# A linear-attention and soft-MoE layer on one core: head pairs projected two at a time on the row halves of TensorE, one rms-normalised form transposed

## The chip, the cores and the metric
One core of a Trainium2 chip. The metric is the device time in microseconds of one execution; lower is better. The kernel has 16 batches of 256 tokens by 128 channels, all in float32 at its borders.

## The reference, cut to what matters
```python
xn = layernorm(x)                                   # (16, 256, 128)
# attention branch
q, k, v = split(xn @ Wqkv + bqkv)                   # 16 heads of 8
feat(t) = exp(clip(t/|t| @ omega * sqrt(2s) - s, -20, 20)) / sqrt(32) * sqrt(w)   # 64 features per head
ctx = causal_sum(qf . kf^T) v;  den = causal_sum(qf . kf^T);  a = ctx / max(den, 1e-6)
# expert branch
xr = rms_norm(xn, gamma_x);  se = rms_norm(slot_embeds, gamma_slot)               # 512 slots
logits = xr @ se^T;  dispatch = softmax over tokens-to-slots;  combine = softmax over slots
slots = dispatch^T @ xr;  h = gelu(slots @ w1);  out = combine @ (h @ w2)
return x + a @ Wout + bout + out
```

## The kernel before, in words
The batches run one after another in `run_rows`, a loop over pairs of batches with the first two and the last two written out. Each engine has its own `row(b, first, nxt, nxt2)`, an order written out by hand over 8 steps `s`. Step s belongs to head pair s of batch b, and beside it the pieces of the previous batch (bp) and the next one (b1) are placed. There is no planner: each engine takes its instructions in program order, and semaphores (`ft_ok`, `cl_ok`, `fe_ok`, ...) join the engines. `after` waits before an instruction; `hold` waits and puts a no-operation behind the wait.

The way of one head pair p: `project` (TensorE, L898) multiplies the stacked, normalised q and k (`stack_t`, 96 rows: high part, low part, high part) by the features' weights (`omega_st[:, p]`) in two matmuls of 256 columns into the one bank `p_feat`. `clip` (VectorE, L681) reads it into `arg`, `feature_exp` (ScalarE, L486) makes `feat`. `scores` (TensorE, L909) multiplies features of keys and queries, head by head on the two row halves, into `p_sa` and `p_sb`. `evac_a` (VectorE, L687) and `evac_b` (ScalarE, L491, then `mask_b` on GpSimd, L428) mask and store them. `context` (TensorE, L926) takes two pairs at a time (a = 0 to 3) into the bank `p_ctx`, where a = 0, 1, 2 add up in one half and a = 3 takes the other; `ctx_copy` (ScalarE, L496) copies each half once.

Because `p_feat` is one bank, each `project(b, p)` waits for the clip of pair p - 1. The projections are spread over the steps: pair 2 in step 0, 3 in step 1, 4 in step 2, 5 in step 3, 6 in step 4, 7 in step 5, and pairs 0 and 1 of the next batch in steps 6 and 7.

Around it in TensorE's order: step 0 `processed(bp)` (h @ w2, L1022), scores 0, `context(bp, 3)`, `transposes(b1)` (L878, L880: the layernormed `xn` and the rms-normalised `xg`, two tiles each), `ctx_transposed(bp)` (L939). Step 1 scores 1, `qkv_product(b1)` (L869), `combine(bp)` (L1032), `attn_back(bp)` (L945, waits for VectorE's `ctx_norm`, L694 to L707). Step 2 scores 2, `attention_out(bp)` (L951), `logits(b)` (L869, 6 matmuls of 512 columns for the tokens' form, 12 of 256 for the slots' form). Step 3 scores 3, `context(b, 0)`, `shift(b)` (L978, L986; needs the maxima of L714 and L720). Step 4 scores 4, `context(b, 1)`, `slot_sums` (L994). Step 5 scores 5, `slots_transposed` (L1002). Step 6 scores 6, `context(b, 2)`, `hidden` half 0 (L869). Step 7 scores 7, `hidden` half 1.

VectorE's order: step 1 `xt_low` (L653), clip 2, evac_a 1, `ctx_norm(bp)`. Step 2 `qkv_bias(b1)` (L661), clip 3, `add_experts(bp)`, evac_a 2, `add_attention(bp)`, `qk_norms(b1)`. Step 3 `token_maxima`, `slot_maxima`, clip 4, evac_a 3, `qk_newton`. Step 4 clip 5, evac_a 4, `ln_stats`. Step 5 clip 6, `slots_norm`, evac_a 5. Step 6 `slots_low` (L735), clip 7, evac_a 6, `ln_apply` of the batch after the next (L636 xn, L640, L647 xg). Step 7 clip 0 of the next batch, evac_a 7.

ScalarE's order in the steps that matter: step 4 `dispatch_exp`, evac_b 4, exp 5, `stack_high` (L479); step 5 `combine_exp`, evac_b 5, exp 6, `ln_root`; step 6 `slots_high` (L513), evac_b 6, exp 7; step 7 two gelus with a table load before and after, `ctx_copy(b, 0)`, exp 0 of the next batch, evac_b 7. SyncE issues the loads of x, the stores and `turn_stack`, a transposing DMA from `stack` to `stack_t`.

Of the kernel before, what the change touches and what calls it, by code (L numbers as in the profile page):

```python
# [16 lines left out]
PAIRS = HEADS // 2  # L17
# [67 lines left out]
def build(nc, x, Wqkv, bqkv, Wout, bout, omega, nodes, weights, gamma_x, gamma_slot, slot_embeds,  # L85
          w1, w2, out):
    with ExitStack() as ctx:
# [23 lines left out]
        gx_bc = sb("gx_bc", [128, 128])  # L111
        gs_bc = sb("gs_bc", [128, 128])
# [8 lines left out]
        node_b = sb("node_b", [32, R])  # L121
        node_b2 = sb("node_b2", [32, R])
        om_scale = sb("om_scale", [32, R])
# [6 lines left out]
        omega_f = sb("omega_f", [32, PAIRS, 128])  # L130
        omega_st = sb("omega_st", [96, PAIRS, 128], F16)

# [6 lines left out]
        xn = sb("xn", [128, TILES, C])  # L139
        junk = sb("junk", [128, NCH, C])  # L140
        xg = sb("xg", [128, 2, TILES, C + 1])
        xt_hi = sb("xt_hi", [128, 2, 512], F32R)
        xt_lo = sb("xt_lo", [128, 2, 512], F32R)
# [3 lines left out]
        stack = sb("stack", [128, 2, 4, TILES, 4, 32], F16)  # L147
        stack_t = sb("stack_t", [128, 2, 2, 4, T], F16)
        vw = sb("vw", [128, 2, TILES, HEADS, 32])
        feat = sb("feat", [128, 4, 2 * T])  # L150
        arg = sb("arg", [128, 2, 2 * T])
        s_sb = sb("s_sb", [128, 4, 2, 384])
        ctx_sb = sb("ctx_sb", [128, 2, T])
        den = sb("den", [128, TILES, HEADS])
# [20 lines left out]
        p_ctx = pb("p_ctx", [128, 2, T])  # L175
# [38 lines left out]
        xn_ok = sem("xn_ok")  # L214
# [18 lines left out]
        ft_ok = sem("ft_ok")  # L233
        cl_ok = sem("cl_ok")
# [7 lines left out]
        cs_ok = sem("cs_ok")  # L242
        ct_ok = sem("ct_ok")
# [30 lines left out]
        def stacked(a):  # L274
            return stack[:, :, :, :, a, :].rearrange("p k g j d -> p j (k g) d")

        def parted():
            return qk_n[:, :, :].rearrange("p j (h d) -> p j h d", d=32)
# [5 lines left out]
        def _(sp):  # L284
            def load_x(b, off):
                hold(sp, xn_ok, count(b, 1, -1))
# [11 lines left out]
            def turn_stack(b):  # L298
                hold(sp, sthi_ok, count(b, 1, 1))
                hold(sp, stlo_ok, count(b, 1, 1))  # L300
                hold(sp, ft_ok, count(b, 8, -8))
                sp.dma_start_transpose(stack_t[:, b[1], :, :, :].rearrange("p k g (j t) -> p (k g j) t", t=128),
                                       stack[:, :, :, :, :, :].rearrange("p k g j a d -> p (k g j a d)")
# [20 lines left out]
            for hl in range(4):  # L324
                for r in range(R):
                    src = omega[r].rearrange("(g q) d m -> q d g m", q=4)[hl]
                    dst = omega_f[8 * hl:8 * hl + 8, :, :].rearrange("d (g u) f -> d g u f", u=2)[
                        :, :, hl // 2, 64 * (hl % 2) + 32 * r:64 * (hl % 2) + 32 * r + 32]
                    sp.dma_start(dst, src).then_inc(d_om, 16)
# [29 lines left out]
        def _(pool):  # L359
            pool.memset(omega_f[:, :, :], 0.0).then_inc(om_zero, 1)  # L360
            pool.memset(stack[:, :, :, :, 3, :], 0.0).then_inc(st_zero, 1)
# [67 lines left out]

            pool.wait_ge(d_bo, 16)  # L430
# [6 lines left out]
            def row(b, first, nxt, nxt2):  # L437
                b1 = step(b, 1)
                for s in range(8):
# [6 lines left out]
                    mask_b(b, s)  # L446
                    if s == 2 and nxt:
# [7 lines left out]
        def _(act):  # L455
# [10 lines left out]
            def xt_high(b):  # L466
                after(act, tr_ok, count(b, 1, 1))
                nc.scalar.activation(xt_hi[:, b[1], :], x01[:, 0, :], ACT.Copy).then_inc(xth_ok, 1)
# [13 lines left out]
            def feature_exp(b, p):  # L482
# [3 lines left out]
                nc.scalar.activation(feat[:, p % 4, :], arg[:, p % 2, :], ACT.Exp, bias=f_bias[:, 0:1]).then_inc(fe_ok, 1)  # L486
# [6 lines left out]
            def ctx_copy(b, g):  # L493
                after(act, cx_ok, count(b, 4, 3 + g))
                after(act, ct_ok, count(b, 1, 0))
                nc.scalar.activation(ctx_sb[:, g, :], p_ctx[:, g, :], ACT.Copy).then_inc(cs_ok, 1)  # L496
# [31 lines left out]
            spread(gx_bc, gamma_x, C).then_inc(d_rows, 16)  # L528
            spread(bqkv_bc, bqkv, 3 * C).then_inc(d_rows, 16)

# [29 lines left out]
            def row(b, first, nxt, nxt2):  # L560

                b1, b2, bp = step(b, 1), step(b, 2), step(b, -1)
                for s in range(8):
# [12 lines left out]
                    if s == 7:  # L576
# [3 lines left out]
                        ctx_copy(b, 0)  # L580
# [14 lines left out]
                    if s == 5 and nxt2:  # L595
                        ln_root(b2)

# [3 lines left out]
            ctx_copy(last_row, 1)  # L601
# [4 lines left out]
        def _(dve):  # L606
# [23 lines left out]
            def ln_apply(b):  # L630
# [3 lines left out]
                after(dve, tr_ok, count(b, 1, 0))  # L634
                for j in range(TILES):
                    last = nc.vector.tensor_scalar(xn[:, j, :], xin[:, b[1], j, :], mv[:, j, 0:1],  # L636
                                                   small[:, VT, j:j + 1], ALU.subtract, ALU.mult)
                last.then_inc(xn_ok, 1)
                for j in range(TILES):
                    last = nc.vector.tensor_scalar(small[:, SG, j:j + 1], small[:, VT, 2 + j:3 + j],  # L640
                                                   small[:, VE, j:j + 1], small[:, VT, j:j + 1], ALU.mult, ALU.mult)
                last.then_inc(sg_ok, 1)
                after(dve, xn_ok, count(b, 1, 1))
                after(dve, sg_ok, count(b, 1, 1))
                after(dve, sl_ok, count(b, 1, -1))
                for j in range(TILES):
                    last = nc.vector.scalar_tensor_tensor(xg[:, b[1], j, 0:C], xn[:, j, :],  # L647
# [491 lines left out]
```

## Time and profile before
| | |
|---|---|
| median of 3 runs | 526.0 us (524.82 to 528.53) |
| the profiled execution, its own time | 524.69 us |
| its span | 523.0 us |
| busy: PE, DVE, ACT, POOL | 474.5, 363.4, 326.0, 176.1 us |

The span runs from the first to the last instruction; the execution's own time is 1.7 us longer. A batch takes about 30.3 us, in two parities (30.1 and 30.5). PE is TensorE's matmuls, DVE VectorE, ACT ScalarE, POOL GpSimd; overlapping records of one engine count once, and a record's own length holds the way through the array, so the distance between two starts is what an instruction occupies.

### The profile page before, as it was taken

To read this page: it belongs to the slowest core of one execution; us is meant where nothing else is said; L and a number is where in the kernel's file an instruction comes from. 1 tells how busy PE (TensorE), PEld (TensorE's weight loads), DVE (VectorE), ACT (ScalarE), POOL (GpSimd) and SP (SyncE) were. 2 spreads that over 40 slices of the span, in tenths; PEclk is the share of its full clock that TensorE was granted. 3 is DMA by queue.
4 is the path that set the end of the run, shared out by engine and by line. 5 is a ranking of instruction groups with operands and counts; after the bars stand their busy time and mean duration, and the time that the engine had idled before them with its cause. 6 is when DMAs were issued, how large, how long until landed. Compare 5 with 4: busy or idle time off the path is not lost.

```text
span 523.0 us, 15293 instructions
## 1 busy us (share of the span) xinstructions
PE 474.5 (91%) x5416; PEld 381.0 (73%) x5416; DVE 363.4 (69%) x937; ACT 326.0 (62%) x560; POOL 176.1 (34%) x278
## 2 busy tenths in 40 slices
PE   3159999999999999999999999999999999999995
PEld 1147787868778786877878687787878778787775
DVE  3778596785859678585958758595875859595551
ACT  2436757486675747667574766757475675847472
POOL 4415142432514243251423335142433415242220
PEclk9999999999999999999999999999999999999999
DMA  2220202020110202011020202002020200202000
GB/s 69 64 51 7 48 11 52 11 55 1 26 36 10 50 10 51 0 34 27 10 50 10 50 0 48 13 10 50 10 50 0 51 9 10 40 12 43 11 2 11
DMA packets 45219, 14.43 MB, mean 28 GB/s; under 512 B 35080, under 2 KB 45064, under 8 KB 45192
## 3 DMA queue, kind: packets, MB, share of 16 engines
q1 hardware_dynamic: 44904, 13.80, 12.3%
q8 instruction: 17, 0.28, 0.2%
q10 hardware_dynamic: 288, 0.26, 0.2%
q14 instruction: 10, 0.08, 0.0%
HBM read 3.57 MB, written 2.10 MB: 11 GB/s over the span
## 4 chain that ended last, share of the span: by engine, by line
PE 68%; DMA 14%; ACT 4%; POOL 4%; issue 4%; SPq 2%; DVE 2%; POOLq 0%; ACTq 0%; DVEq 0%
PE x L869 17%; DMA stack_t<-stack 13%; PE p_sa L909 12%; PE x L1022 11%; PE p_ctx L926 7%; PE x L1032 5%; PE p_feat L898 5%; POOL stack L422 4%; ACT stack L479 4%; PE x L951 2%; PE x L939 2%; PE x L978 2%; PE x L986 1%; PE p_sb L909 1%; PE x L878 1%
## 5 line engine op out<-in xcount | busy, mean ns | idle before, releaser
L428 POOL TENSOR_TENSOR s_sb<-s_sb,causal 128x256 f32<-128x256 f32 x128 | 94.0, 734 | 265.8 <-ACT s_sb L491 264.1
L681 DVE TENSOR_SCALAR arg<-p_feat,f_low,f_high 128x512 f32<-128x512 f32 x128 | 103.1, 806 | 15.7 <-PE p_feat L898 13.3
L687 DVE TENSOR_TENSOR s_sb<-p_sa,causal 128x384 f32<-128x384 f32 x128 | 70.3, 550 | 58.9 <-PE p_sa L909 58.8
L486 ACT ACTIVATE feat<-arg,f_bias 128x512 f32<-128x512 f32 x128 | 91.8, 717 | 21.4 <-DVE arg L681 20.9
L909 PE MATMUL p_sa<-feat 64*64 64x256 f32 (+3 forms) x1024 | 99.1, 310 | 6.6 <-ACT s_sb L491 3.2
L491 ACT ACTIVATE s_sb<-p_sb 128x384 f32<-128x384 f32 x128 | 62.5, 488 | 67.7 <-PE p_sb L909 67.3
L909 PEld LDWEIGHTS p_sa<-feat 64*64 64x64 f32 x1024 | 75.5, 133 | 33.8 <-issue 26.8
L909 PE MATMUL p_sb<-feat 64*64 64x256 f32 (+3 forms) x1024 | 99.1, 311 | 0.0
L909 PEld LDWEIGHTS p_sb<-feat 64*64 64x64 f32 x1024 | 76.2, 133 | 0.0
L898 PE MATMUL p_feat<-stack_t,omega_st 96*128 96x256 f16 x256 | 50.3, 278 | 21.1 <-DMA stack_t<-stack 20.0
L1022 PE MATMUL x<-w_sb,hid_t 128*128 128x128 f32 x512 | 59.8, 275 | 0.0
L1022 PEld LDWEIGHTS x<-w_sb,hid_t 128*128 128x128 f32 x512 | 58.5, 192 | 0.2
L926 PE MATMUL p_ctx<-s_sb,vw 128*32 128x256 f32 (+1 forms) x1024 | 54.9, 332 | 1.2 <-issue 1.2
L898 PEld LDWEIGHTS p_feat<-stack_t,omega_st 96*128 96x128 f16 x256 | 20.1, 99 | 39.2 <-issue 35.6
L518 ACT ACTIVATE hid_t<-x 128x1024 f32<-128x1024 f32 x32 | 32.8, 1025 | 16.2 <-PE x L869 16.0
L926 PEld LDWEIGHTS p_ctx<-s_sb,vw 128*32 128x32 f32 x1024 | 27.5, 109 | 17.0 <-issue 1.9
L1032 PE MATMUL x<-proc,comb_t 128*128 128x129 f32 x256 | 31.2, 274 | 0.0
L994 PE MATMUL x<-xg,disp 128*128 128x129 f32 x256 | 31.2, 274 | 0.0
L994 PEld LDWEIGHTS x<-xg,disp 128*128 128x128 f32 x256 | 29.8, 191 | 0.2
L1032 PEld LDWEIGHTS x<-proc,comb_t 128*128 128x128 f32 x256 | 29.8, 191 | 0.2
L869 PE MATMUL x<-slot_hi,w_hi 128*128 128x512 f32 x64 | 28.6, 447 | 0.0
L501 ACT ACTIVATE attn_t<-x 128x256 f32<-128x256 f32 x16 | 6.2, 385 | 35.3 <-PE x L945 35.3
(137 smaller groups left out, 873.3 us busy)
## 6 DMA issues: line engine op xcount, KB each, us to landing
xin<-in_L_attn_x_dram SPq DMA_DIRECT2D x32, 64.0 KB, 2.4
out_dram<-out_sb SPq DMA_DIRECT2D x32, 64.0 KB, 2.1
se_rows<-n_L_ffn_slot_embeds_dram SPq DMA_DIRECT2D x1, 256.0 KB, 4.1
w_f<-in_L_ffn_w_dram SPq DMA_DIRECT2D x1, 256.0 KB, 4.3
w_sb<-in_L_ffn_w_dram SPq DMA_DIRECT2D x1, 256.0 KB, 4.2
stack_t<-stack SPq DMA_TRANSPOSE x16, 4.4
bqkv_bc<-in_L_attn_bqkv_dram ACTq DMA_DIRECT2D x1, 192.0 KB, 5.0
wqkv_f<-in_L_attn_Wqkv_dram SPq DMA_DIRECT2D x1, 192.0 KB, 4.6
```

The source lines that it names most:

```text
L428: pool.tensor_tensor(v, v, m, ALU.mult).then_inc(mb_ok, 1)
L486: nc.scalar.activation(feat[:, p % 4, :], arg[:, p % 2, :], ACT.Exp, bias=f_bias[:, 0:1]).then_inc(fe_ok, 1)
L491: nc.scalar.activation(s_sb[:, p % 4, 1, :], p_sb[:, 0:384], ACT.Copy).then_inc(eb_ok, 1)
L681: nc.vector.tensor_scalar(arg[:, p % 2, :], p_feat[:, :], f_low[:, 0:1], f_high[:, 0:1], ALU.max, ALU.min).then_inc(cl_ok, 1)
L687: nc.vector.tensor_tensor(s_sb[:, p % 4, 0, :], p_sa[:, 0:384], causal[:, :], ALU.mult).then_inc(ea_ok, 1)
L869: mm = nc.tensor.matmul(dst, a, w, start=start and i == 0, stop=stop and i == 2, skip_group_check=True)
L898: mm = nc.tensor.matmul(p_feat[:, T * k:T * k + T], omega_st[:, p, :], stack_t[0:96, b[1], k, g, :], start=True, stop=True)
L909: mm = nc.tensor.matmul(bank[rows:rows + 64, o:o + hi - lo], f[:, T + keys:T + keys + 64], f[:, lo:hi], start=True, stop=True, skip_group_ ...
L926: mm = nc.tensor.matmul(p_ctx[32 * q:32 * q + 32, a // 3, 128 * kt:T], vw[:, b[1], kt, QUADS * a + q, :], s_sb[:, p % 4, q % 2, T * kt:T * ...
L994: mm = nc.tensor.matmul(x01[:, c // 2, 129 * (c % 2):129 * (c % 2) + 129], disp[:, j, 128 * c:128 * c + 128], xg[:, b[1], j, :], start=(j ...
L1022: mm = nc.tensor.matmul(x01[:, 1, 128 * c:128 * c + 128], hid_t[:, m, 128 * c:128 * c + 128], w2_sb[:, m, :], start=(m == 0 and c == 0), s ...
L1032: mm = nc.tensor.matmul(x23[:, 0, 129 * j:129 * j + 129], comb_t[:, c, 128 * j:128 * j + 128], proc[:, c, :], start=(c == 0), stop=(c == N ...
```

## The change
Six edits, numbered here for the text below.

1. A group g of four heads (pairs 2g and 2g + 1) is projected in one `project(b, g)`: pair 2g on rows 0 to 63 into `p_feat`, pair 2g + 1 on rows 64 to 127 into `p_z`, one matmul of 512 columns each. `stack`, `stack_t` and `omega_st` get a layout of 16 rows a part for it. There are 4 projections a batch where there were 8.
2. `p_ctx` is gone. `context(b, a)` writes into the same bank `p_z`, and so waits for clip 2a + 3; each context is copied by ScalarE (`ctx_copy`, 4 a batch where there were 2), and the next projection waits for that. GpSimd adds the copies (`ctx_sum`, 2 a batch).
3. `arg` has 4 buffers; clip 5 moves from step 4 to step 3.
4. In TensorE's order `context(b, 0)` moves from step 3 to step 2, the logits are cut in two with `project(b, 2)` between them, `slot_sums` is cut in two with `project(b, 3)` between them, project 1 stands in step 1 behind `qkv_product`, and project 0 of the next batch in step 7.
5. `xn` is gone: `ln_apply` writes the rms-normalised form (without gamma_x) into `xg` at once, two transposes are left of four, `xt_hi`/`xt_lo` have 256 columns for 512, gamma_x goes into the slots' scale and into w1, and `qkv_bias` scales the product back by a factor per token.
6. In the head: omega is loaded twice (16 small DMAs, 8 of them on ScalarE's queue, for 8) and gamma_x as a column.

```diff
@@ TensorE
-            def project(b, p):
+            def project(b, g):
                 after(pe, d_st, count(b, 16, 16))
-                after(pe, cl_ok, count(b, 8, p))
-                g = p // 2
-                for k in range(2):
-                    mm = nc.tensor.matmul(p_feat[:, T * k:T * k + T], omega_st[:, p, :],
-                                          stack_t[0:96, b[1], k, g, :], start=True, stop=True)
-                mm.then_inc(ft_ok, 1)
+                after(pe, cs_ok, count(b, 4, g - 1))
+                hold(pe, cl_ok, count(b, 8, 2 * g))
+                for u, (bank, done) in enumerate(((p_feat, ft_ok), (p_z, fz_ok))):
+                    rows = slice(64 * u, 64 * u + 64)
+                    nc.tensor.matmul(bank[:, :], omega_st[rows, g, :],
+                                     stack_t[rows, b[1], :, :, g, :].rearrange("p j k t -> p k j t"), start=True,
+                                     stop=True).then_inc(done, 1)
...
-                if a == 0:
-                    after(pe, cs_ok, count(b, 2, 0))
-                if a == 3:
-                    after(pe, cs_ok, count(b, 2, 1))
+                if a < 3 or nxt:
+                    after(pe, cl_ok, count(b, 8, 2 * a + 4))
...
@@ row of TensorE
-                        project(b, 3)
+                        project(b, 1)
...
                     if s == 2:
+                        context(b, 0)
...
                             attention_out(bp)
-                        project(b, 4)
-                        logits(b, nxt)
+                        logits_tokens(b, nxt)
+                        project(b, 2)
+                        logits_slots(b)
                     if s == 3:
-                        context(b, 0)
                         shift(b)
                     if s == 4:
                         context(b, 1)
-                        project(b, 6)
-                        slot_sums(b)
+                        slot_sums(b, 0)
+                        project(b, 3)
+                        slot_sums(b, 1)
...
                         hidden(b, nxt, 0)
-                        if nxt:
-                            project(b1, 0)
                     if s == 7:
                         hidden(b, nxt, 1)
                         if nxt:
-                            project(b1, 1)
-                    if s in (0, 3, 5):
-                        project(b, s + 2)
+                            project(b1, 0)
@@ VectorE
-                after(dve, ft_ok, count(b, 8, p + 1))
-                after(dve, fe_ok, count(b, 8, p - 1))
-                nc.vector.tensor_scalar(arg[:, p % 2, :], p_feat[:, :], f_low[:, 0:1], f_high[:, 0:1], ALU.max,
+                bank, done = ((p_feat, ft_ok), (p_z, fz_ok))[p % 2]
+                after(dve, done, count(b, 4, p // 2 + 1))
+                after(dve, fe_ok, count(b, 8, p - 3))
+                nc.vector.tensor_scalar(arg[:, p % 4, :], bank[:, :], f_low[:, 0:1], f_high[:, 0:1], ALU.max,
                                         ALU.min).then_inc(cl_ok, 1)
...
-                        clip(b, s + 1)
+                        if s != 4:
+                            clip(b, s + 1)
...
-                    if s == 3 and nxt:
-                        qk_newton(b1)
+                    if s == 3:
+                        clip(b, 5)
+                        if nxt:
+                            qk_newton(b1)
...
-                    last = nc.vector.tensor_tensor(qkv[:, j, :], x01[:, j, 0:384], bqkv_bc[:, :], ALU.add)
+                    last = nc.vector.scalar_tensor_tensor(qkv[:, j, :], x01[:, j, 0:384], small[:, SG, j:j + 1],
+                                                          bqkv_bc[:, :], ALU.mult, ALU.add)
@@ row of ScalarE
-                        ctx_copy(b, 0)
...
                     evac_b(b, s)
+                    if s == 4:
+                        ctx_copy(b, 1)
...
-                            ctx_copy(bp, 1)
+                            ctx_copy(bp, 3)
...
+                    if s in (2, 6):
+                        ctx_copy(b, s // 2 - 1)
@@ row of GpSimd
                     mask_b(b, s)
+                    if s in (4, 6):
+                        ctx_sum(b, s // 2 - 1)
```

## Rows read from the trace of the kernel before
**Rows 1.** The page: span, busy shares, one group of section 5
```profile
span 523.0 us, 15293 instructions
...
PE 474.5 (91%) x5416; PEld 381.0 (73%) x5416; DVE 363.4 (69%) x937; ACT 326.0 (62%) x560; POOL 176.1 (34%) x278
...
L428 POOL TENSOR_TENSOR s_sb<-s_sb,causal 128x256 f32<-128x256 f32 x128 | 94.0, 734 | 265.8 <-ACT s_sb L491 264.1
```

**Rows 2.** Timeline, TensorE, one batch from 209.44: start us, us, engine, line, operation
```profile
209.44 3.74 PE L1022 MATMUL x<-w_sb,hid_t 128*128 128x128 f32 x32
...
216.25 0.38 PE L898 MATMUL p_feat<-stack_t,omega_st 96*128 96x256 f16 x2
...
217.27 0.44 PE L869 MATMUL x<-wqkv_hi,xt_hi 128*128 128x384 f32 x1
...
218.45 0.40 PE L898 MATMUL p_feat<-stack_t,omega_st 96*128 96x256 f16 x2
...
218.68 1.95 PE L1032 MATMUL x<-proc,comb_t 128*128 128x129 f32 x16
...
220.47 0.38 PE L945 MATMUL x<-ident,attn 128*128 128x128 f32 x2
...
221.48 0.71 PE L951 MATMUL x<-wout_sb,attn_t 128*128 128x128 f32 x4
...
222.17 0.48 PE L869 MATMUL x<-se_hi,xt_hi 128*128 128x512 f32 x1
```

**Rows 3.** Timeline, VectorE, same batch, steps 1 to 3
```profile
217.05 0.80 DVE L681 TENSOR_SCALAR arg<-p_feat,f_low,f_high 128x512 f32<-128x512 f32 x1
...
217.77 0.55 DVE L687 TENSOR_TENSOR s_sb<-p_sa,causal 128x384 f32<-128x384 f32 x1
...
218.23 0.25 DVE L694 TENSOR_SCALAR den<-x 128x12 f32<-128x12 f32 x2
...
219.59 1.01 DVE L661 TENSOR_TENSOR qkv<-x,bqkv_bc 128x384 f32<-128x384 f32 x2
...
220.52 0.80 DVE L681 TENSOR_SCALAR arg<-p_feat,f_low,f_high 128x512 f32<-128x512 f32 x1
...
223.84 1.23 DVE L714 TENSOR_REDUCE maxima<-x 128x2 bf16<-128x1024 f32 x1
```

**Rows 4.** Timeline, ScalarE, same batch
```profile
215.32 0.38 ACT L496 ACTIVATE ctx_sb<-p_ctx 128x256 f32<-128x256 f32 x1 [0.52 <-PE p_ctx L926]
...
227.02 0.72 ACT L486 ACTIVATE feat<-arg,f_bias 128x512 f32<-128x512 f32 x1 [0.48 <-DVE arg L681]
...
232.75 0.71 ACT L486 ACTIVATE feat<-arg,f_bias 128x512 f32<-128x512 f32 x1
...
233.70 0.58 ACT L513 ACTIVATE slot_hi<-x 128x512 fp32r<-128x512 f32 x1
```

**Rows 5.** Timeline, VectorE, same batch, step 6
```profile
234.31 0.69 DVE L735 TENSOR_TENSOR slot_lo<-x,slot_hi 128x512 fp32r<-128x512 f32 x1 [1.34 <-ACT slot_hi L513]
...
234.92 0.80 DVE L681 TENSOR_SCALAR arg<-p_feat,f_low,f_high 128x512 f32<-128x512 f32 x1
```

**Rows 6.** Timeline, TensorE, same batch, steps 4 to 7 and the next batch's start
```profile
227.89 0.41 PE L909 MATMUL p_sa<-feat 64*64 64x256 f32 x1
...
227.89 0.43 PE L909 MATMUL p_sb<-feat 64*64 64x256 f32 x1
...
233.60 0.40 PE L909 MATMUL p_sa<-feat 64*64 64x256 f32 x1 [0.17 <-ACT feat L486]
...
234.31 0.86 PE L926 MATMUL p_ctx<-s_sb,vw 128*32 128x256 f32 x16
...
235.09 0.50 PE L869 MATMUL x<-slot_hi,w_hi 128*128 128x512 f32 x1
...
237.13 0.39 PE L898 MATMUL p_feat<-stack_t,omega_st 96*128 96x256 f16 x2 [0.38 <-DMA stack_t<-stack]
...
239.90 1.28 PE L1022 MATMUL x<-w_sb,hid_t 128*128 128x128 f32 x10
```

More of the change, by code:

```diff
@@ L16 @@
 R, M = 2, 32
-PAIRS = HEADS // 2
+GROUPS = HEADS // 4
 QUADS = 4
@@ L274, in stacked, with load_omega @@
         def stacked(a):
-            return stack[:, :, :, :, a, :].rearrange("p k g j d -> p j (k g) d")
+            return stack[:, :, :, :, :, a, :].rearrange("p j k g u d -> p (j k g u) d")
         def parted():
-            return qk_n[:, :, :].rearrange("p j (h d) -> p j h d", d=32)
+            return qk_n[:, :, :].rearrange("p j (h d) -> p (j h) d", d=16)
+        def load_omega(eng, a):
+            for u in range(2):
+                for h in range(2):
+                    row = 64 * u + 16 * a + HD * h
+                    for r in range(R):
+                        col = 64 * h + 32 * r
+                        eng.dma_start(omega_f[row:row + HD, :, col:col + 32],
+                                      omega[r].rearrange("(g q) d m -> q d g m", q=4)[2 * u + h]).then_inc(d_om, 16)
         block = ctx.enter_context(nc.Block())
@@ L323, in _ @@
             sp.wait_ge(om_zero, 1)
[L324 to L329, printed above, removed]
+            load_omega(sp, 0)
             load_x((0, 1), T)
@@ L428, in mask_b, with ctx_sum @@
                 pool.tensor_tensor(v, v, m, ALU.mult).then_inc(mb_ok, 1)
+            def ctx_sum(b, a):
+                hold(pool, cs_ok, count(b, 4, a + 1))
+                hold(pool, cd_ok, count(b, 2, a - 1))
+                pool.tensor_tensor(ctx_sb[:, 0, :], ctx_sb[:, 0, :], ctx_part[:, a - 1, :], ALU.add).then_inc(cd_ok, 1)
             pool.wait_ge(d_bo, 16)
@@ L491, in evac_b, with ctx_copy @@
                 nc.scalar.activation(s_sb[:, p % 4, 1, :], p_sb[:, 0:384], ACT.Copy).then_inc(eb_ok, 1)
[L493 to L496, printed above, removed]
+            def ctx_copy(b, a):
+                after(act, cx_ok, count(b, 4, a + 1))
+                if a % 3 == 0:
+                    after(act, ct_ok, count(b, 1, 0))
+                    to = ctx_sb[:, a // 3, :]
+                else:
+                    after(act, cd_ok, count(b, 2, 0))
+                    to = ctx_part[:, a - 1, :]
+                nc.scalar.activation(to, p_z[:, 0:T], ACT.Copy).then_inc(cs_ok, 1)
             def attn_copy(b):
@@ L600, in _ @@
             proc_copy(last_row)
-            ctx_copy(last_row, 1)
+            ctx_copy(last_row, 3)
             attn_copy(last_row)
@@ L874, in transposes @@
                 after(pe, xg_ok, count(b, 1, 1))
[L875 removed]
                 after(pe, ge_ok, count(b, 2, -3))
                 for j in range(TILES):
[L878 to L881 removed]
+                    mm = nc.tensor.transpose(x01[:, 0, 128 * j:128 * j + 128], xg[:, b[1], j, 0:C], ident[:, :])
                 mm.then_inc(tr_ok, 1)
@@ L933, in ctx_transposed @@
             def ctx_transposed(b):
-                after(pe, cs_ok, count(b, 2, 2))
+                after(pe, cs_ok, count(b, 4, 4))
+                after(pe, cd_ok, count(b, 2, 2))
                 after(pe, ge_ok, count(b, 2, 2))
```

122 lines of the change are left out of this document (62 added, 60 removed).

## The prediction
> **What bounds the kernel now.** I read the page first, then the timeline of each engine over one batch in the middle. TensorE is busy for 474.5 of 523.0 us, VectorE and ScalarE for two thirds of it [rows 1], so by shares TensorE is the bound. The timeline says more: from one `processed` at 209.44 to the next at 239.90 a batch takes 30.46 us [rows 2, 6], and TensorE's gaps are short, 0.17 us before scores 6 for ScalarE's exp and 0.38 us before the projection of the next batch for the DMA of `stack_t` [rows 6]. But the reader should see how close the other engines follow: exp 4 ends at 227.74 and scores 4 start at 227.89 [rows 4, 6]; `attn_back` starts at 220.47, 0.88 us after VectorE turned from `ctx_norm` to `qkv_bias` [rows 2, 3]; clip 7 ends at 235.72, when `hidden` is already running [rows 5, 6]. TensorE is full because the clips are done long before they are needed. So a change that saves array time but orders TensorE behind late clips is paid on another engine's clock. I therefore recost one batch as a chain, on the time scale of these rows, and multiply.
>
> **Array time saved.** Two matmuls of 256 columns occupy 0.23 us (218.45 to 218.68 [rows 2]), 0.32 ahead of scores (216.25 to 216.57, when scores 1 begin; 217.27 less the 0.70 they take). The new pair moves 512 columns on each row half. If the halves run side by side, as `p_sa` and `p_sb` do (both at 227.89 [rows 6]), one `project` costs 0.23, and 4 replace 8: about 1.1 us a batch. If they run one behind the other it is 0.45 each and nothing is saved. I take side by side, being the nearest row. Two of four transposes go, 0.3 us of array time, but the next piece, `ctx_transposed`, needs the copy of the context that ends at 215.70 [rows 4], after the transposes as it is; I count 0 (bounds 0 and 0.3).
>
> The Trainium skill (TensorEngine Tiling (Array Packing), Key Properties) says that tiles in different row halves run in parallel, and also that changing the tiling mode, not just the tile, drains TensorE. That speaks against the change, since none of the 8 old projections used row halves of full width. The rows bear out a cost of 0.09 us at a switch (0.32 against 0.23). By that rule each new projection would pay it twice, 0.7 us a batch at most, of which only what is on the chain counts.
>
> **Start of the batch, to projection 1.** `ctx_copy(b, 0)` no longer stands ahead of exp 0, evac_b 7 and so mask_b 7, for which context 3 waits: 0.28 us gained (0 to 0.38, the copy's length [rows 4]). Project 2 is gone from before scores 1: 0.32 gained. `xt_low`, half as wide, hides. So project 1, behind `qkv_product` as project 3 was, starts at 218.45 - 0.60 = 217.85.
>
> **Steps 1 and 2, the first new waits.** Before, clip 2 ran at 217.05 [rows 3], because pair 2 had been projected in step 0. Now it must wait for project 1: 217.85 + 0.43 (the two matmuls' record is 0.40 long [rows 2]) = 218.28. Queued behind it on VectorE are evac_a 1, `ctx_norm(bp)`, `qkv_bias(b1)` and clip 3. Their distances are in [rows 3]: clip 0.72, evac_a 0.46, `ctx_norm` 1.36, `qkv_bias` 0.93. So `ctx_norm` starts at 219.46 and is done at about 220.95. TensorE, after project 0.23 and `combine` 1.79 [rows 2], stands before `attn_back` at 219.87 and waits 1.1 us (bounds 0.8 and 1.4). Scores 2 then run from 221.26 to 221.96. `context(b, 0)` now waits for clip 3, since both use `p_z`: 220.82 + 0.93 + 0.80 + 0.05 = 222.60, a wait of 0.6 (0.3 to 0.9; `qkv_bias` with a per-token scale may cost 0.1 more). Context takes 0.78 (234.31 to 235.09 [rows 6]). `attention_out` starts at 223.38, and the logits, which came 0.69 after it with project 4 between them (some 0.14), at 223.93 in place of 222.17 [rows 2]: 1.76 late. That context 0 left step 3 gives nothing back, since from the maxima on VectorE sets the pace.
>
> **Steps 3 to 5.** Token maxima 1.76 later than 223.84 [rows 3]: 225.60. From their start to scores 4 it was 4.05 us, all of it maxima, clip 4 and exp 4 (exp 227.02 to 227.74 [rows 4]); so scores 4 start at 229.65. Where context 0 used to cover this chain, TensorE now waits (about 0.2 before `shift`, 0.4 before scores 4). Clip 5 in step 3 comes after clip 4 and delays `qk_newton` by 0.7; GpSimd's and ScalarE's `stack` work behind it has as much slack. ScalarE's order from scores 4 to exp 6 took 4.86 (227.89 to 232.75 [rows 4, 6]). It gets `ctx_copy(b, 1)` (0.28 of its time, and a wait for context 1), while it had 0.48 free ahead of evac_b 5; I add 0.14 (0 to 0.4). Exp 6 starts at 234.65, scores 6 at 235.50, done at 236.21.
>
> **Step 6, the largest wait.** `context(b, 2)` now waits for clip 7, and clip 7 stands on VectorE behind `slots_low`, which waits for ScalarE's `slots_high`, which stands behind exp 6. In the rows that is exp 6 at 232.75, `slots_high` 233.70, `slots_low` 234.31, clip 7 from 234.92 to 235.72 [rows 4, 5]: 2.97 us from exp 6. So context 2 starts at 237.67, and TensorE has waited 1.46 us (1.2 to 1.6). Before, it ran at 234.31, ahead of clip 7 [rows 5, 6]. `hidden` starts at 238.45 in place of 235.09: 3.36 late.
>
> **Step 7.** From `hidden` to the next `processed` it took 4.81 (235.09 to 239.90). One project and the wait for the DMA (0.33 + 0.38) go, as project 0 now comes after both halves and the DMA, started 1.9 late, still lands before: 4.10. The next batch starts at 242.55. Clip 0 and clip 1 have the 3.7 us of `processed` for themselves [rows 2], so evac_a 7, queued behind clip 0, hurts nobody. SyncE's queue: the store waits for `add_attention` about 1.8 later, `turn_stack` behind it still waits longest for `stack`. GpSimd's two `ctx_sum` cost 0.73 each (the size of a mask [rows 1]) on an engine one third busy; they lie beside its waits.
>
> **The sum.** 242.55 - 239.90 = +2.65 us a batch (VectorE loses 0.7 and 0.3 us of work for `xn` and the half-wide `xt_low`, but not where it is waited for). There are 14 such periods between the 15 times `processed` opens a batch: +37.1. The first batch has no `ctx_norm` to wait for but the waits of steps 2 and 6, +2.9, less 0.6 for shorter preparation of omega in the head; its extra DMAs on ScalarE's queue lie beside the load of x. The last has no `qkv_bias`, so about +1.8. Total +41.2 on the profiled 524.7: 565.9. The median of the runs stands 1.3 above the profiled one; I keep 566.
>
> **The rivals.**
> Other side: the array is what counts. If the clips were done when TensorE arrives, that is if the three chains were shorter by 1.1, 0.6 and 1.5 us, the 0.6 of the start and the 0.7 of step 7 would remain: -1.3 x 16 = -21, 505. For it: TensorE is 91% busy [rows 1]. Against: the distances in [rows 3 to 5] are fixed orders on one queue. Chance 0.04.
> Only step 6 bites: VectorE absorbs the first chain. Then -0.6 at the start, +0.14, +1.46, -0.71: +0.3 a batch, 530. Against it is the distance from project to `ctx_norm`'s end, 3.1 us against 2.0 of cover. Chance 0.07.
> Only steps 1 and 2 bite: ScalarE takes `slots_high` early enough. Then 2.65 - 1.46 = +1.2, about 544. Chance 0.10.
> The halves don't overlap or drain, and the waits breed more: 0.22 more for each of the two projections on the chain (1 and 0), so +3.1, about 573. The saving the change's name promises would be absent. For it: no row shows 64 rows by 128 columns. Chance 0.19.
> My forecast: 0.60.
>
> **How the numbers follow.** A measurement tells about 1% from no change here. Faster by over 1% is the first rival, 0.04. Within 1% is half or so of the second, 0.05. The rest, 0.91, is slower. The range leaves out 505 and 530 below and a fall-out above: the waits' bounds add up to -0.8 and +0.9 a batch, 552 to 580, and 544 is a case of its own; I take 544 to 579.
>
> **What would show it.** In the profile after: TensorE's waits before `attn_back` on VectorE's `attn` (about 1.1 us, 15 times), before `context` on `arg` (0.6 and 1.5, some 15 times each), before scores 4; the wait on the DMA of `stack_t` gone but for the first; the new matmuls on `p_feat` and `p_z` starting within 0.02 us of each other; TensorE's share down from 91% to about 82%; a batch of 33 us. I am wrong if context 2 starts at once behind scores 6, or if clip 2 begins before `combine` does.

## The result, and the profile after
The changed kernel takes 591.97 us (median of 4 runs, 588.7 to 594.62) against 526.4 us: 1.124 times the time before (95% interval 1.120 to 1.127). The forecast was 566 us, 544 to 579: right in sign and in the waits that it names, too small by 26 us, and the result is outside its range.

The page of the changed kernel, the lines that answer to [rows 1]:

```profile
span 590.7 us, 15290 instructions
...
PE 489.2 (83%) x5256; PEld 369.6 (63%) x5256; DVE 357.5 (61%) x905; ACT 336.4 (57%) x592; POOL 195.4 (33%) x310
...
PEclk8558899999989999999989999999989999998999
...
L436 POOL TENSOR_TENSOR s_sb<-s_sb,causal 128x256 f32<-128x256 f32 x128 | 93.1, 727 | 257.2 <-ACT s_sb L506 257.1
...
L441 POOL TENSOR_TENSOR ctx_sb<-ctx_sb,ctx_part 128x256 f32<-128x256 f32 x32 | 23.4, 731 | 26.8 <-ACT ctx_part L516 26.8
```

TensorE is busy for 83% where it was 91%. Its granted clock (PEclk, in tenths of full speed) shows 5s in the first slices and 8s later on. The 8s are new, the 5s only beyond 37 us. The page of the kernel before reads 9 in its first slices too, but its own matmuls tell otherwise: of the same form, 384 columns, one takes 0.52 us at 14.49 and 0.34 us at 37.58 (and the next one starts 0.32 us later at first, 0.18 us later then), and in the changed kernel's head it takes 0.53 us. So in the kernel before, too, the head ran at half clock, up to about 37 us:

```profile
14.49 0.52 PE L869 MATMUL x<-wqkv_lo,xt_hi 128*128 128x384 f32 x1
...
37.58 0.34 PE L869 MATMUL x<-wqkv_lo,xt_hi 128*128 128x384 f32 x1
```

GpSimd's additions cost 0.73 us each, and no wait on them is in the list.

Who made TensorE wait (columns: waiter, releaser: us in total, times, longest us):

```profile
PE p_z L952 <- DVE arg L705: 28.7, 29, 1.4
PE p_feat L926 <- DMA stack_t<-stack: 18.9, 1, 18.9
PE p_sa L937 <- ACT feat L501: 16.0, 33, 1.7
PE x L972 <- DVE attn L731: 10.8, 15, 0.8
```

The DMA of `stack_t` is down to the one wait of the head, as forecast. New are 29 waits of `context` for clips and 15 of `attn_back` for `ctx_norm`. Scores wait 33 times for an exp, 16.0 us in all, where it was 16 times and 2.7 us. One batch at full clock, TensorE's timeline, which answers to [rows 2, 6]:

```profile
205.12 0.39 PE L926 MATMUL p_feat<-stack_t,omega_st 64*128 64x512 f16 x1
205.12 0.39 PE L926 MATMUL p_z<-stack_t,omega_st 64*128 64x512 f16 x1
205.44 3.84 PE L1053 MATMUL x<-w_sb,hid_t 128*128 128x128 f32 x32
...
213.81 0.39 PE L926 MATMUL p_feat<-stack_t,omega_st 64*128 64x512 f16 x1
...
214.13 2.05 PE L1063 MATMUL x<-proc,comb_t 128*128 128x129 f32 x16
216.83 0.44 PE L972 MATMUL x<-ident,attn 128*128 128x128 f32 x2 [0.65 <-DVE attn L731]
...
218.59 0.86 PE L952 MATMUL p_z<-s_sb,vw 128*32 128x256 f32 x16 [0.63 <-DVE arg L705]
...
219.85 0.47 PE L900 MATMUL x<-se_hi,xt_hi 128*128 128x512 f32 x1
...
225.78 0.40 PE L937 MATMUL p_sa<-feat 64*64 64x256 f32 x1 [0.50 <-ACT feat L501]
...
231.89 0.40 PE L937 MATMUL p_sa<-feat 64*64 64x256 f32 x1 [0.39 <-ACT feat L501]
...
234.05 0.86 PE L952 MATMUL p_z<-s_sb,vw 128*32 128x256 f32 x16 [1.39 <-DVE arg L705]
...
239.06 3.17 PE L1053 MATMUL x<-w_sb,hid_t 128*128 128x128 f32 x26
```

and VectorE in the same batch, which answers to [rows 3, 5]:

```profile
214.23 0.81 DVE L705 TENSOR_SCALAR arg<-p_feat,f_low,f_high 128x512 f32<-128x512 f32 x1 [2.21 <-PE p_feat L926]
...
217.74 0.80 DVE L705 TENSOR_SCALAR arg<-p_z,f_low,f_high 128x512 f32<-128x512 f32 x1
...
221.52 1.22 DVE L738 TENSOR_REDUCE maxima<-x 128x2 bf16<-128x1024 f32 x1
...
224.08 0.80 DVE L705 TENSOR_SCALAR arg<-p_feat,f_low,f_high 128x512 f32<-128x512 f32 x1
...
232.59 0.69 DVE L759 TENSOR_TENSOR slot_lo<-x,slot_hi 128x512 fp32r<-128x512 f32 x1 [1.34 <-ACT slot_hi L533]
233.20 0.80 DVE L705 TENSOR_SCALAR arg<-p_z,f_low,f_high 128x512 f32<-128x512 f32 x1
```

A batch is 33.62 us here (205.44 to 239.06), and 33.9 in the other parity (batches alternate between two lengths). Clip 2 starts at 214.23, 0.42 after project 1, and all that stood behind it follows; `context(b, 0)` starts 0.05 after clip 3 ends (217.74 + 0.80), `context(b, 2)` 0.05 after clip 7 ends (233.20 + 0.80).

The windows view shows what the forecast left out (columns: stretch, us, busy time of each engine with its count, granted clock, DMA share, GB/s). The first two lines are whole batches, the last two stretches inside the second one:

```profile
core 0: us, PE busy (x) PEld busy (x) DVE busy (x) ACT busy (x) POOL busy (x), PEclk, DMA share, GB/s
171.60:205.50 33.90, 29.57 (x331) 22.49 (x329) 21.72 (x55) 20.71 (x37) 11.81 (x18) 1.00 0.11 23
136.50:171.60 35.10, 31.03 (x331) 23.27 (x329) 21.72 (x55) 20.68 (x37) 11.82 (x18) 0.95 0.11 24
163.80:165.00 1.20, 0.00 (x0) 0.00 (x0) 1.20 (x3) 0.43 (x1) 0.62 (x1) 0.97 1.16 214
165.00:168.30 3.30, 3.25 (x20) 2.09 (x21) 1.82 (x8) 2.38 (x3) 0.83 (x2) 0.50 0.43 94
```

In the middle of that batch TensorE is idle, waiting for clip 7, and at 165.0 its clock falls to half (1.2 of 2.4 GHz) for 3.3 us. The batch takes 35.1 us, where batches of its parity without a fall take 33.6 (the one at 205.44). Four of the 14 batches between the first and the last `processed` that opens a batch are like this (35.11, 35.12, 35.14, 34.94 us). The same wait stands in the other batches, in which the clock did not fall.

### The profile page after: what moved, and what is told of

It reads as the page before. It is cut to its first block, busy times and chain, and to the rows that moved or that the text cites. A ratio compares the mean times of both kernels' runs of the same rounds, so it can differ in the third digit from the quotient of the medians.

```text
span 590.7 us, 15290 instructions
## 1 busy us (share of the span) xinstructions
PE 489.2 (83%) x5256; PEld 369.6 (63%) x5256; DVE 357.5 (61%) x905; ACT 336.4 (57%) x592; POOL 195.4 (33%) x310
## 4 chain that ended last, share of the span: by engine, by line
PE 59%; DVE 16%; issue 10%; ACT 9%; DMA 2%; SPq 2%; POOL 1%; DVEq 1%; ACTq 0%; POOLq 0%
PE x L900 19%; PE x L1053 10%; PE p_z L952 8%; PE p_sa L937 7%; DVE arg L705 6%; PE x L1024 6%; ACT feat L501 5%; PE p_feat L926 3%; DVE qkv L683 2%; PE x L966 2%; PE x L978 2%; ACT s_sb L506 2%; DVE s_sb L711 1%; DVE maxima L738 1%; ACT slot_hi L533 1%
## 5 line engine op out<-in xcount | busy, mean ns | idle before, releaser
L705 DVE TENSOR_SCALAR arg<-p_feat,f_low,f_high 128x512 f32<-128x512 f32 x64 | 51.7, 808 | 102.9 <-PE p_feat L926 101.8
L506 ACT ACTIVATE s_sb<-p_sb 128x384 f32<-128x384 f32 x128 | 62.3, 487 | 76.2 <-PE p_sb L937 74.7
L952 PE MATMUL p_z<-s_sb,vw 128*32 128x256 f32 (+1 forms) x1024 | 58.5, 349 | 31.6 <-DVE arg L705 28.7
L1053 PE MATMUL x<-w_sb,hid_t 128*128 128x128 f32 x512 | 61.3, 278 | 0.0
L952 PEld LDWEIGHTS p_z<-s_sb,vw 128*32 128x32 f32 x1024 | 28.3, 113 | 50.8 <-DVE arg L705 27.8
L705 DVE TENSOR_SCALAR arg<-p_z,f_low,f_high 128x512 f32<-128x512 f32 x64 | 51.3, 801 | 0.0
L926 PE MATMUL p_feat<-stack_t,omega_st 64*128 64x512 f16 x64 | 25.0, 390 | 18.9 <-DMA stack_t<-stack 18.9
L1024 PE MATMUL x<-xg,disp 128*128 128x129 f32 x256 | 37.1, 287 | 0.0
L407 POOL TENSOR_TENSOR qk_sq<-qkv 128x512 f32<-128x512 f32 x16 | 16.6, 1040 | 58.9 <-DVE qkv L683 58.9
L1063 PE MATMUL x<-proc,comb_t 128*128 128x129 f32 x256 | 32.7, 280 | 0.0
L441 POOL TENSOR_TENSOR ctx_sb<-ctx_sb,ctx_part 128x256 f32<-128x256 f32 x32 | 23.4, 731 | 26.8 <-ACT ctx_part L516 26.8
L1063 PEld LDWEIGHTS x<-proc,comb_t 128*128 128x128 f32 x256 | 29.8, 191 | 3.4 <-issue 3.4
```

What stands on the lines that cost most here:

```text
L506: nc.scalar.activation(s_sb[:, p % 4, 1, :], p_sb[:, 0:384], ACT.Copy).then_inc(eb_ok, 1)
L705: nc.vector.tensor_scalar(arg[:, p % 4, :], bank[:, :], f_low[:, 0:1], f_high[:, 0:1], ALU.max, ALU.min).then_inc(cl_ok, 1)
L926: nc.tensor.matmul(bank[:, :], omega_st[rows, g, :], stack_t[rows, b[1], :, :, g, :].rearrange("p j k t -> p k j t"), start=True, stop=Tru ...
L952: mm = nc.tensor.matmul(p_z[32 * q:32 * q + 32, 128 * kt:T], vw[:, b[1], kt, QUADS * a + q, :], s_sb[:, p % 4, q % 2, T * kt:T * kt + T - ...
L1024: mm = nc.tensor.matmul(x01[:, half, 129 * (c % 2):129 * (c % 2) + 129], disp[:, j, 128 * c:128 * c + 128], xg[:, b[1], j, :], start=(j == ...
L1053: mm = nc.tensor.matmul(x01[:, 1, 128 * c:128 * c + 128], hid_t[:, m, 128 * c:128 * c + 128], w2_sb[:, m, :], start=(m == 0 and c == 0), s ...
```

## The experiments
The starts of `processed` in each timeline give three parts: the head and first batch, the middle batches, the rest. They carry most of what follows, and are of one profiled execution each. The first one has some chance in it: with the head as the change has it, the first projection starts anywhere from 30.7 to 32.2 us, as the loads land. Each ratio is to the kernel before as it ran again beside that kernel (526.1 to 526.5 us).

| kernel | median us | ratio to before (95%) | first `processed` at | a middle batch |
|---|---|---|---|---|
| before | 526.4 | | 58.0 | 29.8 to 30.6 |
| changed | 592.0 | 1.120 to 1.127 | 68.7 | 33.6 to 33.9, four 34.9 to 35.1 |
| clip 7 earlier | 560.7 | 1.062 to 1.069 | 64.1 | 32.2 to 32.4 |
| project 1 earlier | 567.1 | 1.073 to 1.080 | 64.4 | six 31.6 to 32.0, eight 33.3 to 33.5 |
| both | 530.7 | 1.005 to 1.010 | 61.1 | 30.4 to 30.5 |
| both, clip 3 earlier | 530.8 | 1.005 to 1.010 | 61.2 | 30.4 to 30.5 |
| before, rms form alone | 525.7 | 0.997 to 1.000 | 60.8 | 29.7 to 30.6 |
| both, full-row projections | 529.0 | 1.003 to 1.007 | 62.3 | 30.3 to 30.4 |
| both, projections twice | 544.1 | 1.030 to 1.036 | 61.9 | 31.3 to 31.4 |
| both, bias loaded first | 526.3 | 0.999 to 1.002 | 56.6 | 30.4 to 30.5 |
| last version | 522.1 | 0.990 to 0.993 | 56.1 | 30.1 to 30.3 |
| the same on row halves | 523.2 | 0.992 to 0.996 | 56.7 | 30.1 to 30.3 |
| before, bias loaded first | 525.7 | 0.997 to 1.001 | 57.9 | 29.8 to 30.5, one 30.9, one 32.3 |

### Clip 7 earlier
```diff
@@ row of VectorE
-                        if s != 4:
+                        if s not in (4, 6):
                             clip(b, s + 1)
...
+                    if s == 5:
+                        clip(b, 7)
```


> The changed kernel with clip 7 moved on VectorE from step 6, behind slots_low, to the end of step 5, as clip 5 already is; nothing else differs. Theory (waits behind late clips): context 2 no longer waits 1.39 us in each of 16 batches, -21 us; and since the clock's falls to 1.2 GHz begin in that wait (each costs 1.2 us, four of them) they go or move, -5 us: about 566 us. Rival (the array: switches between row halves and full rows, and the copies on ScalarE, set the pace): context 2 starts earlier but hidden then waits for slots_low, 2 to 6 us less, 586 to 590 us.

560.66 us, 31.3 less. The middle batches lose 1.52 us at full clock (33.80 to 32.28 on average), and no batch is stretched any more, so the theory holds, and in the middle its size too (21 us of waits and 5 of clock). It left out the head: the first `processed` comes 4.6 us earlier. Of these, 1.5 are there before any clip (the first projection starts at 30.7 in place of 32.2); in the rest the clock falls once before `processed` in place of twice. The wait list of this run has 15 waits on clips in place of 29, 9.7 us in place of 28.7 (the longest 0.7).

### Project 1 earlier
```diff
@@ row of TensorE
                     if s == 0:
...
+                        project(b, 1)
                     if s == 1:
                         if nxt:
                             qkv_product(b1)
-                        project(b, 1)
```


> The changed kernel with project 1 moved on TensorE from step 1, behind qkv_product, to the end of step 0, where pair 2 was projected before the change. Theory: clip 2 runs 1.9 us earlier, so attn_back no longer waits for ctx_norm (0.65 us and what the weight load adds, 0.9 together) nor context 0 for clip 3 (0.63): -1.5 us a batch, about -23 us, 569 us. Rival: clip 3 stands behind qkv_bias whatever project 1 does, so only the first wait goes and the second grows by it: 0 to -3 us.

567.13 us, 24.8 less. The wait for `attn` is off the list and 15 waits on clips are left, those of `context(b, 2)`, 1.4 us at the longest. At full clock a batch takes 31.88 us on average, 1.92 less than the changed kernel, more than the 1.5 expected. The rival falls. But eight batches of 14 are 1.5 us longer at a lower clock (columns as in the windows above):

```profile
64.40:97.80 33.40, 30.51 (x330) 23.48 (x328) 21.90 (x55) 20.29 (x37) 11.87 (x18) 0.95 0.12 25
97.80:129.80 32.00, 29.13 (x331) 22.50 (x329) 21.77 (x55) 20.42 (x37) 11.90 (x18) 1.00 0.13 27
```

In the kernel with the other move, whose longest waits of TensorE in the middle batches are 0.7 and 0.8 us, no middle batch is stretched. That the falls go with the wait of 1.4 us is what these three kernels agree on; none of them changed the wait without changing the time. A fourth case stands under the head.

### Both moves


> Both moves together. Theory: the two waits lie on the same chain one after the other, so the gains add: -2.9 us a batch and the clock's falls gone, 592 - 46 - 5 = 541 us. Rival (a second limit close behind, as the maxima-clip 4-exp 4 chain or ScalarE's): they add up to less than two thirds, 555 us or more.

530.71 us. In the middle batches the two gains add to within 0.1 us: 33.80 (the mean of the ten at full clock) - 1.52 - 1.92 = 30.36, measured 30.44. The rival, a second limit close behind, falls. The forecast was 541, with 2.9 us less in each of 16 batches. The middle batches at full clock lose 3.4, which makes 6 us, and the first `processed` comes 7.6 us earlier in place of 2.9, which makes 5; the last batches give 1 back. The clock is at full in all middle batches, as forecast.

```profile
219.82 0.39 PE L928 MATMUL p_feat<-stack_t,omega_st 64*128 64x512 f16 x1
...
220.14 0.43 PE L939 MATMUL p_sa<-feat 64*64 64x256 f32 x1
...
223.78 0.38 PE L974 MATMUL x<-ident,attn 128*128 128x128 f32 x2
...
224.80 0.86 PE L954 MATMUL p_z<-s_sb,vw 128*32 128x256 f32 x16
...
231.99 0.40 PE L939 MATMUL p_sa<-feat 64*64 64x256 f32 x1 [0.50 <-ACT feat L501]
```

`attn_back` (223.78) and `context(b, 0)` (224.80) have no idle time before them. What is left is 0.50 us before scores 4 for exp 4 and 0.39 us before scores 6 for exp 6: 32 waits, 14.2 us in all, where the kernel before had 2.7 us of them (and some 0.36 us a batch before a projection, for the DMA of `stack_t`, which is gone).

The windows view also says what the new projections are worth on the array. Over the 14 middle batches TensorE is busy for 408.3 us before, for 405.7 with the rms form alone (further below) and for 406.0 with both moves. So the rms form takes 2.6 us off, and the projections in pairs nothing more.

### Clip 3 earlier, beside both moves
```diff
@@ row of VectorE
+                    if s == 1:
+                        clip(b, 3)
```
(and clip 3 is left out of step 2). 

> Both moves, and clip 3 taken on VectorE from step 2, behind qkv_bias, to the end of step 1. Theory: in the run with both moves context 0 does not wait any more, so this changes nothing (within 3 us of it). Rival: clip 3 behind qkv_bias still holds context 0 by up to 0.4 us a batch, then 6 us less.

530.75 us: no difference. Once project 1 is early, clip 3 behind `qkv_bias` holds nobody.

### The rms form alone, on the kernel before
The diff is edit 5 of the change. 

> The kernel before with edit 5 alone: one rms-normalised form, two transposes in place of four, xt_hi and xt_lo with 256 columns, the product of q, k and v scaled back in qkv_bias. Projections, p_ctx and all orders as before. Theory: nothing of it lies where TensorE waits (the next piece waits for the copy of the context as it is), so within 2 us of 526. Rival: the array time of the two transposes (0.3 us a batch) is gained whole: 521 to 522 us.

525.66 us, 0.998 of before (0.997 to 1.000). Two transposes and some 0.5 us of VectorE's busy time a batch (354.6 us in place of 363.4 over the whole span) are worth 0.07 us a batch (30.18 against 30.25 on average). So this part neither caused the loss in the middle batches nor could have paid for it. In its profile, though, the first `processed` comes 2.8 us later than before; the whole time doesn't show it.

### Full-row projections, and projections twice
```diff
@@ full rows: omega_st has a second copy in which the other half's rows are zero
-                    rows = slice(64 * u, 64 * u + 64)
-                    nc.tensor.matmul(bank[:, :], omega_st[rows, g, :],
-                                     stack_t[rows, b[1], :, :, g, :]
+                    nc.tensor.matmul(bank[:, :], omega_st[:, u, g, :],
+                                     stack_t[:, b[1], :, :, g, :]
```


> The kernel with both moves (530.7 us), with each group's two projections made by full matmuls of 128 rows (the other half's weights are zero) in place of 64 rows each: same banks, same semaphores, no switch of the row halves. The stream of a pair of projections is 0.43 us in place of 0.21. Theory, from the profile after the change (a project occupies 0.32 us, and the groups around it 0.1 longer each): what the halves save in the stream the switch takes back, so within 4 us of 530.7. Rival: the halves save what they promise, 0.2 us at three places a batch on TensorE's path: 540 us.

528.98 us, 1.7 less than with the row halves. The intervals of the two ratios, 1.003 to 1.007 and 1.005 to 1.010, overlap, so the times alone don't settle it; in the profiles a middle batch is 0.11 us shorter, 30.32 against 30.44. The other run issues the pair of matmuls twice. 

> The kernel with both moves, each pair of projections issued twice (the same result written twice). It measures the pair itself without the switch. If the halves run side by side: 0.21 us for each of the three or four projections on TensorE's path, 9 to 13 us more, 540 to 544 us, and in the timeline a project occupies 0.53 in place of 0.32. Rival (one behind the other): twice that, 549 to 558 us.

544.05 us. A middle batch is 0.87 us longer, four times 0.22. Both together say what a projection on the row halves costs between full-row work. TensorE's timelines around project 0 of the next batch; first the row halves, twice:

```profile
217.91 0.39 PE L928 MATMUL p_feat<-stack_t,omega_st 64*128 64x512 f16 x1
217.91 0.39 PE L928 MATMUL p_z<-stack_t,omega_st 64*128 64x512 f16 x1
218.13 0.38 PE L933 MATMUL p_feat<-stack_t,omega_st 64*128 64x512 f16 x1
...
218.44 3.84 PE L1060 MATMUL x<-w_sb,hid_t 128*128 128x128 f32 x32
222.21 0.43 PE L944 MATMUL p_sa<-feat 64*64 64x256 f32 x1
```

then full rows:

```profile
213.45 0.39 PE L930 MATMUL p_feat<-stack_t,omega_st 128*128 128x512 f16 x1
213.68 0.38 PE L930 MATMUL p_z<-stack_t,omega_st 128*128 128x512 f16 x1
213.90 3.73 PE L1057 MATMUL x<-w_sb,hid_t 128*128 128x128 f32 x32
217.56 0.43 PE L941 MATMUL p_sa<-feat 64*64 64x256 f32 x1
```

The halves do run side by side (both at 217.91), and a second pair costs 0.22 (217.91 to 218.13). But from the last pair to `processed` it is 0.31, and `processed` then takes 3.77 to the next scores against 3.66 behind full rows. Ahead of the pair there is another 0.08 (with both moves the last matmul of `hidden` starts at 212.68 and project 0 at 213.00, 0.32 in place of 0.24). So a pair on row halves costs 0.22 and 0.28 at its borders, 0.50; two full-row matmuls cost 0.45. Here the saving in the stream is all paid back in the switch. The other places, with both moves against full rows: around project 2 halves cost 0.08 us more (0.87 against 0.79 from the last matmul of the tokens' logits to the second of the slots'), around project 3 they cost 0.09 more (2.50 against 2.41 for `slot_sums` with the project in it). At project 1, which stands right before scores, themselves on row halves, they cost 0.12 less (0.90 against 1.02 from `ctx_transposed` to scores 1).

### The head
```diff
@@ SyncE
             sp.dma_start(wqkv_f[:, :], Wqkv).then_inc(d_qkv, 16)
+            spread(bout_bc, bout, C).then_inc(d_bo, 16)
```
(and gone from its place behind omega's loads). On the kernel with both moves: 

> The kernel with both moves, with the load of the output's bias, for which GpSimd waits before it squares q and k of the first batch, issued on SyncE's queue before omega's eight loads, not after them. Theory: the head is longer after the change because this load landed at 18.1 us in place of 16.2 (eight more loads of omega, and theirs ahead of it); now q and k (done at 13.9) set the time: 4 us less, 527 us. Rival: omega's own loads set the head's end, no change.

526.34 us, 4.4 less, as expected; the first `processed` starts 4.5 us earlier and the middle is unchanged. The control, the same on the kernel before: 

> The kernel before with the bias loaded first, nothing else: the control for the two runs above. There the bias landed at 16.2 us and q and k were done at 15.9, so GpSimd gains 0.9 us at most: 525 to 526 us. Rival (the head's gain has nothing to do with the change): 4 us less, 522 us.

525.68 us, 0.999 of before (0.997 to 1.001): the gain does not come from the early load alone. It exists where the first batch's q and k are ready early (13.9 us after the change, 15.9 before) and this load comes late, which is the changed kernel's head.

This control happens to say something about the clock too. In its first whole batch the projection behind `hidden` half 0 waits 1.55 us for the DMA of `stack_t`, where the same wait in the profile of the kernel before is 0.46 us; and here, in a kernel without any wait for a late clip, the clock fell to half at 88.1 for 3.4 us. That batch takes 32.3 us (30.2 in the profile of before), the next one 30.9.

```profile
86.45 0.39 PE L898 MATMUL p_feat<-stack_t,omega_st 96*128 96x256 f16 x2 [1.55 <-DMA stack_t<-stack]
88.10:91.50 3.40, 3.40 (x14) 2.63 (x13) 0.86 (x2) 1.52 (x2) 0.00 (x0) 0.50 0.00 0
```

and in the kernel before:

```profile
85.41 0.39 PE L898 MATMUL p_feat<-stack_t,omega_st 96*128 96x256 f16 x2 [0.46 <-DMA stack_t<-stack]
```

### The last version
Both moves, the bias first, full-row projections, and
```diff
@@ row of ScalarE
+                    if s == 5:
+                        feature_exp(b, 6)
                     evac_b(b, s)
...
-                    if 0 < s < 7:
+                    if 0 < s < 7 and s != 5:
                         feature_exp(b, s + 1)
```


> The kernel with both moves, the bias loaded first (526.3 us) and full-row projections (1.7 us less than halves where it was run), and on ScalarE in step 5 exp 6 ahead of evac_b 5. Theory: scores 6 wait 0.39 us for exp 6, which stands behind evac_b 5 although clip 6 is long done; with the swap they wait only for evac_b 5, 0.4 to 0.5 us a batch less: 517 to 519 us, faster than both kernels. Rival: slots_high, behind the later evac_b 5, then holds hidden, and nothing is gained: 524 to 525 us.

522.09 us, 0.9915 of before (0.990 to 0.993): 0.8% faster than the kernel before, a small gain but clear of the noise, and 3 to 5 us more than the forecast. Scores 6 now wait 0.18 us for evac_b 5 where they waited 0.39 for exp 6, and the middle batches gain 0.1 us against full-row projections without the swap (30.23 against 30.32), not 0.4: ScalarE's evac_b 5 comes last where exp 6 did. The waits of 0.50 for exp 4 and 0.30 for the slots stay.

```profile
230.82 0.66 PE L1039 MATMUL x<-ident,slot_v 128*128 128x128 f32 x4 [0.30 <-DVE slot_v L757]
231.66 0.40 PE L943 MATMUL p_sa<-feat 64*64 64x256 f32 x1 [0.18 <-ACT s_sb L507]
```

With row halves instead: 

> The same as the run before it with the projections on the row halves, as the change has them. Theory: 1.5 to 3 us more than it (the switch costs 0.05 to 0.1 us a projection more than the stream it saves): 519 to 521 us. Rival: the halves are the cheaper form once TensorE is better fed: less than it.

523.15 us. The difference, 1.1 us, has the expected sign and is smaller than expected. The intervals of the ratios (0.990 to 0.993, 0.992 to 0.996) overlap a little, though the slowest of the six runs on full rows (522.31) is below the fastest of the six on halves (522.87).

## Why the prediction was wrong in size
By its own steps, on the batch that opens at 205.44 (times from there, forecast against measured):

- Project 1: 8.41 against 8.37. `attn_back`: 11.51 against 11.39. `context(b, 0)`: 13.16 against 13.15. First logits: 14.49 against 14.41. Token maxima: 16.16 against 16.08. The first two waits were right in place. In size, `attn_back` came 0.91 us behind the end of `combine`'s usual 1.79 us (0.65 of it stands as idle time), where I had 1.1; `context(b, 0)` waited 0.63, where I had 0.64.
- Scores 4: 20.21 against 20.34. Clip 4 came 2.56 us after the start of the maxima (221.52 to 224.08) where it had come 2.34 after, and the slots' logits now end behind one more project.
- Exp 6: 25.21 against 25.59, so 5.25 from scores 4 where I had 5.00. I had put the addition on ScalarE's copy. It is on TensorE: from scores 4 to scores 5 it was 3.60 and is 3.99, with `slot_sums` cut in two around a switch of the row halves, and evac_b 5 and exp 6 wait for scores 5.
- `context(b, 2)`: 28.23 against 28.61, that is 3.02 from exp 6 as forecast. The largest wait was right (1.39 where I had 1.46).
- To the next `processed`: 33.11 against 33.62, the last 0.13 from the project ahead of `processed`.

The first step that failed is the price of a `project`: "If the halves run side by side, ... one `project` costs 0.23, and 4 replace 8: about 1.1 us a batch." The halves do run side by side, but between full-row work a project costs 0.50, so 4 cost about what 8 did (8 x 0.23 is 1.84, 4 x 0.50 is 2.0, a little less for the one beside scores). The busy time of TensorE agrees: the pairs took nothing off it (405.7 us with the rms form alone, 406.0 with both moves). The working knew of a switch, but priced it at 0.09 from one row, 0.18 for the two borders of a project, and put none of it into the forecast; measured, the two borders cost 0.28. The Trainium skill (TensorEngine Tiling (Array Packing), Key Properties) says that a change of tiling mode drains TensorE. The cost at both borders agrees with that; no run here shows that it is a drain. With this and the maxima the middle batches are 33.6 to 33.9 us at full clock against a forecast of 33.1 (and 30.25 before on average, where I had taken the longer parity, 30.46, on both sides): (33.80 - 30.25) x 14 = 50 us in place of 37.

The second is what I didn't have at all: the clock. All waits were priced as idle time. Beside the wait for clip 7 the granted clock fell to 1.2 GHz in four middle batches, 1.1 to 1.5 us each, 5 us.

The third is the head, "+2.9, less 0.6": the first `processed` came 10.7 us later, not 2.3. The output's bias landed at 18.1 in place of 16.2, and GpSimd squares nothing before it. Only 0.7 us of that are the eight more loads of omega ahead of it (it is issued at 12.4 in place of 11.7). The rest is the load's own time, 5.7 us for 4.5, which differs from run to run: it took 4.9 with both moves, and 5.6 with the rms form alone, which has only the eight old loads. The DMA of `stack_t` landed at 32.1, not 30.1. After that the granted clock stayed at half to 42 us, where the kernel before was at full from 37, and fell again near 45 and at 62.5 (there behind 1.5 us in which `context` waited for GpSimd's mask), as the windows view of the changed kernel's first batch shows up to 60 us (columns as in the windows above):

```profile
36.00:42.00 6.00, 4.78 (x38) 3.62 (x31) 1.99 (x4) 1.86 (x4) 1.46 (x2) 0.50 0.00 0
42.00:45.00 3.00, 1.16 (x19) 0.71 (x18) 2.58 (x5) 0.73 (x2) 0.11 (x1) 0.99 0.00 0
45.00:49.00 4.00, 3.38 (x21) 2.25 (x22) 2.29 (x4) 1.99 (x5) 3.01 (x7) 0.57 0.01 4
49.00:60.00 11.00, 9.74 (x119) 7.25 (x119) 9.06 (x20) 6.83 (x13) 5.00 (x6) 1.00 0.01 1
```

Of the 10.7 us the bias explains 4.5 (the run with it first), the two waits and the clock with them 7.6 (both moves); they sum to more than 10.7 because with all three the head is 1.4 us shorter than that of the kernel before (56.6 against 58.0). Some of the 7.6 is chance: the bias landed 0.7 us earlier in that run and the first projection started 1.4 us earlier, without any change to either. How much of the rest is edit 5, whose head alone came 2.8 later in its profile, stays open.

Sum: 50 + 5 + 10.7 + 2.1 for the end (43.6 us from the last such start, 41.5 before; forecast 1.8) = 68, the difference of the spans, 590.7 - 523.0. The rivals of the forecast: "Only step 6 bites" and "Only steps 1 and 2 bite" are refuted by the two moves, each worth its own part. The rival on the array's side is refuted too, in an instructive way: with the waits for clips and for `attn` gone the kernel takes 530.7, not 505. The array's saving was not there, and 0.9 us a batch of waits for exp 4 and exp 6 came in its place. "The halves don't overlap or drain" was half right: they overlap, but the switch takes back what that saves. So of the 26 us that were missing, 13 are in the middle batches at full clock, 5 are the clock's falls in them, and 8 are the head.

What stays open is what makes the clock fall. In the traces kept here, every fall before the last microseconds comes during an idle stretch of TensorE or within 1.7 us of its end, and these stretches were 1.2 to 1.9 us long, from whatever cause (a clip, GpSimd's mask, the DMA of `stack_t` in the control of the head). The runs whose longest stretch in the middle batches was 0.5 to 0.8 us show no fall there. But many such stretches were followed by no fall, and no run held everything else fixed and filled the wait with other work.

## What to carry to other kernels
Where two producers come to share a bank, write down for each new wait what is queued ahead of the releaser on its engine: here the clip that freed the bank stood behind a chain through ScalarE, and moving two instructions in program order gave back 61 of 66 us, the clock's part with it. An engine that is 91% busy in the array has no claim to be the only bound; its consumers' order may be what keeps it full. And a switch of the array's tiling has a price at both borders, so small matmuls should change it seldom: for 512 columns between full-row work it cost more than running side by side saved (0.50 us against 0.45), and beside scores, which are on row halves already, it did not.

## What the runs showed of the hardware
A pair of 64-row fp16 matmuls of 512 columns on the two row halves occupies TensorE for 0.22 us when repeated, and 0.50 when it stands alone between full-row work; two 128-row matmuls of the same shape 0.45. The granted clock fell to half for 3.3 us beside a stretch with TensorE idle for 1.2 to 1.4 us in a batch that was otherwise busy at 1.0, and did so in four of the 14 middle batches, near 165, 301, 438 and 540 us; with project 1 earlier and the same wait, in eight of 14. In the kernel before with the bias loaded first it did so once, 1.7 us after a wait of 1.55 us. In the head of the kernel before, matmuls ran at the length of half clock (0.52 us for 0.34) although the page shows no lower clock there.
